# The first projection of a mixture of experts by Strassen's scheme: 42 short matmuls in place of 24 long ones

## The reference, cut to what matters

```python
x = x + xattn(layernorm(x), ctx, ...)                      # first part: not changed
t = layer_norm(layernorm(x).reshape(-1, 512), gamma, beta) # 16384 tokens, 512 wide
logits = t @ gate_weight.T                                 # 8 experts
top1 = argmax(logits)                                      # and the rank of a token in its expert
dispatch[top1, slot] += t * keep                           # (8, 1024, 512): at most 1024 tokens an expert
h = gelu(einsum('ech,ehi->eci', dispatch, wi))             # wi: (8, 512, 2048)   first projection
expert_out = einsum('eci,eih->ech', h, wo)                 # wo: (8, 2048, 512)   second projection
x = x + (residual + weight * expert_out[top1, slot])
```

## Time and profile before

| | |
|---|---|
| Median of 3 runs | 3422.04 us (3421.35 to 3423.3) |
| The profiled execution's own time | 3423.79 us |
| Its span | 3422.0 us |
| PE busy | 3297.7 us (96%), 15632 matmuls |
| DVE busy | 2557.8 us (75%) |
| ACT busy | 1773.7 us (52%) |
| POOL busy | 1383.0 us (40%) |

### The profile page before, as it was taken

How to read it: one execution, slowest core, us unless ns; L and a number is a source line. 1 busy time by engine, 2 the same in 40 slices (tenths; PEclk the granted TensorE clock), 3 DMA queues, 4 the chain that set the end, 5 groups by cost and what they waited for, 6 DMA issues and landing times. The chain is left out here.

```text
span 3422.0 us, 48582 instructions
## 1 busy us (share of the span) xinstructions
PE 3297.7 (96%) x15632; PEld 2611.4 (76%) x15632; DVE 2557.8 (75%) x3185; ACT 1773.7 (52%) x3622; POOL 1383.0 (40%) x1608
## 2 busy tenths in 40 slices
PE   6999999999999999999999589999999999999998
PEld 5777777777777777777777368888888888888886
DVE  4999999999999999999999644444444444444443
ACT  5666666676766666666666343333333333333332
POOL 3476767676776767676775500000000000000000
PEclk9999999999999999999999789999999999999999
DMA  6422222222121222212130232333333333233231
GB/s 226 148 100 75 88 74 63 76 72 86 62 86 62 93 68 86 87 62 74 62 100 31 76 130 99 111 124 115 118 123 120 113 123 110 98 111 113 97 110 37
DMA packets 223806, 325.82 MB, mean 95 GB/s; under 512 B 37104, under 2 KB 103024, under 8 KB 223728
## 3 DMA queue, kind: packets, MB, share of 16 engines
q1 hardware_dynamic: 208368, 307.85, 26.7%
q0 software_dynamic: 15360, 16.99, 1.5%
HBM read 256.70 MB, written 101.97 MB: 105 GB/s over the span
## 5 line engine op out<-in xcount | busy, mean ns | idle before, releaser
L1458 ACT ACTIVATE act<-hid_ps 128x512 f32<-128x512 f32 x256 | 153.1, 598 | 796.3 <-PE hid_ps L1385 796.3
L1339 POOL TENSOR_TENSOR tally<-tally,unit 1x1 f32<-1x1 f32 x16 | 2.9, 180 | 1348.2 <-DVE mixed L1531 1348.2
L1519 DVE CAST act_h<-act 128x512 fp32r<-128x512 f32 x256 | 109.2, 427 | 522.0 <-ACT act L1458 522.0
L1385 PE MATMUL hid_ps<-tok_h,w_h 128*128 128x512 f32 x1024 | 404.9, 395 | 0.0
L1385 PE MATMUL hid_ps<-tok_l,w_h 128*128 128x512 f32 x1024 | 399.3, 390 | 0.0
L1385 PE MATMUL hid_ps<-tok_h,w_l 128*128 128x512 f32 x1024 | 398.7, 389 | 0.0
L1401 PE MATMUL out_ps<-w_l,act_h 128*128 128x512 f32 x1024 | 398.5, 389 | 0.0
L1399 PE MATMUL out_ps<-w_h,act_h 128*128 128x512 f32 x1024 | 398.3, 389 | 0.0
L1400 PE MATMUL out_ps<-w_h,act_l 128*128 128x512 f32 x1024 | 398.3, 389 | 0.0
L1513 DVE TENSOR_TENSOR w_l<-w_raw,w_h 128x2048 fp32r<-128x2048 f32 x128 | 293.4, 2293 | 90.9 <-ACT w_h L1452 90.9
L1452 ACT ACTIVATE w_h<-w_raw 128x2048 fp32r<-128x2048 f32 x128 | 244.5, 1910 | 8.9 <-PEq L311 8.9
(11 more groups left out here) (196 smaller groups left out, 8762.2 us busy)
## 6 DMA issues: line engine op xcount, KB each, us to landing
w_raw<-in_L_ffn_wi SPq DMA_DIRECT2D x128, 512.0 KB, 3.6
w_raw<-in_L_ffn_wo SPq DMA_DIRECT2D x128, 512.0 KB, 4.5
w_raw<-in_x SPq DMA_DIRECT2D x32, 1024.0 KB, 5.1
w_raw<-in_ctx SPq DMA_DIRECT2D x32, 1024.0 KB, 5.2
x_res<-in_x SPq DMA_DIRECT2D x31, 1024.0 KB, 5.3
out<-x_res SPq DMA_DIRECT2D x31, 1024.0 KB, 4.4
slots<-rows SPq DMA_DIRECT2D x4, 4160.0 KB, 16.0
got<-slots SPq DMA_DIRECT2D x15, 1040.0 KB, 7.4
```

The source lines that it names most:

```text
L1339: nc.gpsimd.tensor_tensor(tally[:], tally[:], unit[:], ALU.add).then_inc(tallied, 1)
L1385: last = nc.tensor.matmul(hid_ps[i % 2][:], a[:, c, :], b[:, c, :], start=first_, stop=last_)
L1458: nc.scalar.activation(act32[i % 2][:], hid_ps[i % 2][:], ACT.Gelu).then_inc(gelu, 1)
L1519: v.tensor_copy(act_h[i % 4][:], act32[i % 2][:]).then_inc(ah_ready, 1)
```

## The change

The first projection of a group now goes in 8 steps of 256 inner columns. The weights of a step and the tokens are cut into 2x2 blocks, each 128 inner columns (of the two halves of the 2048) by 256 of the contraction, and 256 of the contraction by 256 tokens. Strassen's scheme (in the form with 15 additions) forms four sums of weight blocks, `S1` to `S4`, and four of token blocks, `T1` to `T4`, and takes seven block products in place of eight. A product is 2 blocks of the contraction by 3 terms, that is 6 matmuls of 256 columns. The products accumulate in four banks, `x_ps`, `y_ps`, `w_ps` and `v_ps`; where a partial sum is needed twice, ACT copies it from bank to bank (`seed_x`, `seed_w`) or to memory (`keep_fifth`), and DVE makes two last additions (`add_22`, `add_12`). The transposes go through one bank, shared with `v_ps`, in place of two. ACT makes all high parts, DVE all low parts. `mixed` goes; the result is written over `res`, and the columns for the scatter come by a small transfer of their own (`meta_of`).

For a step `q` the PE list is: `P1`, `P5`, then `P4` of step q-1, `down` tile 0 of step q-2, `P6`, `P2`, `down` tile 1, `P7`, `P3`, `down` tiles 2 and 3. A tile of `down` is now 6 matmuls of 512 columns, since a step has 256 inner columns.

```diff
-ISTEPS = INNER // P
-PAIRS = ISTEPS // 2
+HALF = INNER // 2
+STEPS = HALF // P
+TOK = GROUP // 2
+INNER_RING = 2
+BLOCKS = 7
@@ load_weights
+    for h in range(2):
+        at = h * HALF + k * P
+        sp.dma_start(raw[:, 0, h * 512:(h + 1) * 512].rearrange("p (c n) -> p c n", c=CB),
+                     wi[bass.ds(e, 1), :, at:at + P].rearrange("a (c p) n -> p (a c) n", p=P)).then_inc(raw_in[k % 2], 16)
@@ PE
+                def product(dst, q, i, a, b, start=False):
+                    g, w = i // STEPS, i % 2
+                    for k in range(2):
+                        for x, y in ((wi_h, tok_h), (wi_l, tok_h), (wi_h, tok_l)):
+                            last = nc.tensor.matmul(dst, x[w][:, a, k, :], y[g][:, b, k, :],
+                                                    start=start and k == 0 and x is wi_h and y is tok_h, stop=False,
+                                                    skip_group_check=True)
+                    return last
...
+                def first_products(q, n, i):
...
+                    pe.wait_ge(wi_low, q * 2 + 2)
+                    wait(pe, sum12, q)
...
+                    product(y_ps, q, i, A11, B11, start=True).then_inc(p1_mm, 1)
...
+                    product(v_ps, q, i, S1, T1, start=True).then_inc(p5_mm, 1)
+                def last_product(q, i):
+                    pe.wait_ge(sum22, q + 1)
+                    product(w_ps, q, i, A22, T4).then_inc(p4_mm, 1)
+                def sixth_product(q, i):
+                    pe.wait_ge(seeded_x, q + 1)
+                    product(y_ps, q, i, S2, T2).then_inc(p6_mm, 1)
+                def second_product(q, i):
+                    product(x_ps, q, i, A12, B21).then_inc(p2_mm, 1)
+                def late_products(q, i):
+                    pe.wait_ge(seeded_w, q + 1)
+                    product(w_ps, q, i, S3, T3).then_inc(p7_mm, 1)
+                    product(y_ps, q, i, S4, B22).then_inc(p3_mm, 1)
@@ ACT, one step
+                    seed_x(q, i)                     # x_ps <- y_ps, 256 columns
+                    keep_fifth(q, i)                 # fifth <- v_ps, 256
+                    inner_high(q - 1, before, 0)     # 512
+                    gelu_21(q - 1)                   # 256
+                    inner_high(q - 1, before, 1)     # 512
+                    weights_high(q + 1, after)       # 768
+                    seed_w(q, i)                     # w_ps <- y_ps, 256
+                    gelu_11(q)                       # 256
+                    weight_sums_high(q + 1, after)   # 1024
+                    down_weights_high(q + 1, after)  # 1024
+                    gelu_22(q)                       # 256
+                    gelu_12(q)                       # 256
+                    if j == 0:
+                        norm(n + 1, 1 - g)           # 4 x 512
+                    if 1 <= j <= CB:
+                        affine(n + 1, j - 1)         # 512
+                    if j == 3:
+                        tokens_high(n + 1, 1 - g, 0) # 1024
+                    if j == 4:
+                        residual(n, g, (0, 1, 2))    # 3 x 512
+                    if j == 5:
+                        tokens_high(n + 1, 1 - g, 1) # 512
+                        tokens_high(n + 1, 1 - g, 2) # 1024
+                        residual(n, g, (3,))         # 512
+                    if j == 6:
+                        tokens_high(n + 1, 1 - g, 3) # 1024
@@ DVE, one step
+                    weights_add(q + 1, after, 0)     # 2 x 256
+                    weights_add(q + 1, after, 1)     # 2 x 256
+                    inner_low(q - 1, before, 0)      # 512
+                    if j == 2:
+                        mix(n - 1, 1 - g, (2, 3))    # 2 x 512
+                    if on(q):
+                        if j == 4:
+                            tokens_low(n + 1, 1 - g, 0)  # 1024
+                        if j == 5:
+                            tokens_add(n + 1)            # 4 x 512
+                        if j == 6:
+                            tokens_low(n + 1, 1 - g, 1)  # 512
+                            tokens_low(n + 1, 1 - g, 2)  # 1024
+                        if j == 7:
+                            tokens_low(n + 1, 1 - g, 3)  # 1024
+                    inner_low(q - 1, before, 1)      # 512
+                    if j == 1:
+                        mix(n - 1, 1 - g, (0,))      # 512
+                    weights_low(q + 1, after)        # 768
+                    weight_sums_low(q + 1, after)    # 1024
+                    add_22(q, i)                     # 256
+                    add_12(q, i)                     # 256
+                    down_weights_low(q + 1, after)   # 1024
+                    if j == 1:
+                        mix(n - 1, 1 - g, (1,))      # 512
```

More of the change, by code:

```diff
@@ L1354, in _, with mark_banks, turn @@
             def _(pe):
-                def turn(e, g, c):
-                    n = group(e, g)
+                def mark_banks():
+                    for bank in (x_bank, w_bank):
+                        for a in range(2):
+                            nc.tensor.matmul(bank[:, a * P:(a + 1) * P], eye[:], eye[:],
+                                             start=(a == 0), stop=True, skip_group_check=True)
+                def turn(n, c, q):
+                    if not group_on(n):
+                        return
                     first = isinstance(n, int) and n == 0
@@ new lines, in _ @@
+                weights_high(0, 0)
+                weight_sums_high(0, 0)
+                down_weights_high(0, 0)
+                norm(0, 0)
+                affine(0, 0)
+                affine(0, 1)
+                affine(0, 2)
+                affine(0, 3)
+                tokens_high(0, 0, 0)
+                tokens_high(0, 0, 1)
+                tokens_high(0, 0, 2)
+                tokens_high(0, 0, 3)
+                for i in range(16):
+                    step(0, i)
+                with act.Fori(1, EXPERTS - 1) as e:
+                    for i in range(16):
+                        step(e, i)
@@ L1498, in _ @@
+                for i in range(16):
+                    step(EXPERTS - 1, i)
+                step(EXPERTS, 0)
             @block.vector
@@ new lines, in _ @@
+                weights_add(0, 0, 0)
+                weights_add(0, 0, 1)
+                weights_low(0, 0)
+                weight_sums_low(0, 0)
+                down_weights_low(0, 0)
+                tokens_low(0, 0, 0)
+                tokens_add(0)
+                tokens_low(0, 0, 1)
+                tokens_low(0, 0, 2)
+                tokens_low(0, 0, 3)
+                for i in range(16):
+                    step(0, i)
+                with dve.Fori(1, EXPERTS - 1) as e:
+                    for i in range(16):
+                        step(e, i)
@@ L1560 @@
+                for i in range(16):
+                    step(EXPERTS - 1, i)
+                for i in range(3):
+                    step(EXPERTS, i)
 def kernel(**inputs):
```

523 lines of the change are left out of this document (337 added, 186 removed).

## The result

The kernel before took 3422.04 us (median of 13 runs on the same chip), the changed one 3416.04 us (13 runs, 3411.25 to 3419.26). One run of the kernel before was a slow one, at 3732.36 us; the other twelve lie between 3421.35 and 3424.19, and the ratio uses fast runs alone. The ratio is 0.9979, with a 95% interval of 0.9971 to 0.9986: faster by 0.2%, where 1.7% was forecast (3363 us, range 3338 to 3412). Of the 59 us that were forecast 6 came. The profiled run took 3416.19 us, its span is 3414.4; the earlier trace rows have 3422.0.

The account below looks back on a forecast made before the run. The prediction took PE's sum of matmul pitches as the bound: 3422.0 - 69.1 (shorter steps) + 12 (start) - 2 (end) = 3362.9, so 3363 us, range 3338 to 3412.

Parts of the forecast that it names:

- the likeliest case: Experts' part: PE's pitch, 0.1133 to 0.125 us for 256 columns, sets the time, all else hidden; 3345 to 3407, chance 0.75.
- Nothing waits: Experts' part: PE has no gap; 384 matmuls make 87.05 of a group's 89.05 us, so only PE's sum counts.
- p, the pitch of 256 columns: Short fp32r matmuls on PE: 0.1167 us each, between readings of 0.1133 and 0.1200, saving 69.1 us over 128 steps.
- Change between 256 and 512 columns costs nothing that I can see.: PE's row changes between short and long matmuls: each length keeps its own pitch, at no cost.
- The 2.0 us left for transposes: Each group on PE: 16 transposes and what they disturb take 2.0 us, before and after the change.
- The start: Ahead of the first product: serial lists make it 9.0 us late, with later waits and half clock 12 us more.
- The end: After the last matmul: one mix is left in place of four, 2.0 us less.
- ACT and DVE hidden: Experts' part: ACT takes 8.05 and DVE 8.56 of a 10.34 us step, so both stay under PE.
- the wait at step 5: Step 5 of a group: add_12 ends at 10.4 against 10.34 us; costed at nothing, at most 8 us.
- Rival 2: Experts' part: the order on ACT and DVE becomes the bound; for example 48 us lost, 3411; chance 0.12.
- Rivals 3 and 4: Short matmuls: weight load not hidden, 3747 us, chance 0.09; or bare stream at 0.110 us, 3327 us, chance 0.04.
- The estimate of 0.1092 us: Short matmuls on PE: pitch by the skill's formula N / 2.4 + 2.5 ns, which would save 109 us.

Follow-up runs that it names:

- e1: The changed kernel with the loop over experts 1 to 6 written out on SP, PE, ACT and DVE: 3393.89 us.
- e5: The changed kernel with the loop over experts written out on PE alone: 3391.97 us.
- e6: The changed kernel with the loop kept on PE alone, written out on ACT, DVE and SP: 3416.48 us.
- e11: The changed kernel, loops kept, with 32 unused 8x8 matmuls put ahead of the experts' part: 3397.97 us.
- e13: As e11, and in an expert's last step two late products go ahead of the second down tile, so 18 long matmuls end the loop's body: 3394.18 us.
- e4: The kernel before, loops written out, each 512-column matmul of the first projection cut into two of 256 columns: 3464.81 us.
- e10: The kernel before, loops written out, each 512-column matmul of the first projection cut into four of 128 columns: 4124.28 us.
- e7: As e1, with P6 and P2 moved ahead of down tile 0, so a step has two rows of long matmuls, not three: 3391.79 us.
- e12: The changed kernel, loops kept, with 64 unused 8x8 matmuls put ahead of the experts' part: 3414.42 us.

## Why the prediction was wrong

The side was right (0.86 for faster), and the likeliest case was the right mechanism: PE's sum of pitches, with ACT and DVE hidden. The time lies outside the range of 3338 to 3412. Of the 51.5 us between 3414.4 and the forecast span of 3362.9, 22.7 lie in the plain groups, 22.8 in the turns and 6.0 in the start.

- **A term that was not there: the turn of the loop** (22.8 us). This is the step that failed. "Nothing waits: this part is the sum of PE's pitches, and only that sum, or a wait that the change makes, can move its end" looked for waits between engines and in transfers. The change also makes PE's loop longer, 1088 pairs for 800, and that was never counted, though both counts follow from its own numbers (48 and 66 matmuls a step). e1, e5 and e6 show the place, e11 to e13 both gaps. Shown. Without the turns the changed kernel takes 3393.89 us (e1), inside the range; the other misses, 28.7 us together, would not have left it.
- **p, the pitch of 256 columns**, taken at 0.1167 as "the middle of the two likely readings". It is the upper reading, 0.120: 336 x 3.7 ns = 1.22 us a group, 19.5 us. The fp32 rows, of which it says "That speaks for growth with the columns", misled; the note that fp32r is another mode was the better guide. A middle between two readings of which one must be true is a value that neither gives. Shown by e4.
- **"Change between 256 and 512 columns costs nothing that I can see."** The long ones average 0.2302 in place of 0.2267: 192 x 3.5 ns = 0.68 us a group, 10.9 us. Seen in every trace with mixed rows, e4 too; its cause is open.
- **The 2.0 us left for transposes** were 1.42, and 0.48 that belonged to the long ones near them; in the sum this gives 7.7 us back (16 x 0.48, against the 1.90 of a plain group before).
- **The start**, 12 us forecast, 18.0 measured. The lists up to the first product were right within about 1 us (8.0 for 9.0). The table load (1.28 us) and the wait of the second step for its sums of weights were not laid out. The end was right.
- **ACT and DVE hidden**: right. ACT is busy 70% of the long window (78% forecast), DVE 71% (83%), PE waits for neither after 2012 us, and the wait at step 5, costed at nothing, costs nothing. Rival 2 falls. The sum for ACT had a slip: the list of a step has seven instructions of 256 columns, not six, so it should have read 6.77 and with the group's share 8.43 of 10.34 us. That both engines were busy for less than their sums fits the overlap of neighbours by some 0.08 us, which the forecast had read from `mix`. (The worth of the change at p = 0.125 is 24.3 us, not 24.6; nothing hangs on it.)
- **Rivals 3 and 4**: the load is hidden at 256 columns and is the bound at 128 (e10); no short matmul is at 0.110. The estimate of 0.1092 us that the forecast worked out from the Trainium skill (TensorE: Matmul & The Clock Gate, section Back-to-back issue gap), which gives the formula for an isolated matmul, does not hold for this format; 0.120 does.

## What to carry to other kernels

Before replacing long instructions by more and shorter ones in a loop, count the instructions of the loop's body on that engine, and ask whether it still fits: here 800 pairs did and 1088 did not. A long branch at the loop's end and traffic on the instruction queue between its turns show in a trace that it does not. If it must be fetched again, end the body with instructions long enough that those already queued cover the branch (here 17 x 0.2267 us for 3.6), and have its first instructions not at the end of a piece; or write the loop out. With that, the change is worth 0.9% (e5, 3391.97 us; e7 the same) and not 0.2%; with the loop kept and only moved and reordered, it is worth 0.8% (e13).

## What the runs showed of the hardware

- 64 unused pairs of load and matmul far ahead of a loop made the kernel some 18 us faster (e11), 128 of them changed nothing that can be told (e12: ratio 0.9979, as without them), by where the loop then lay.
- Of the ten gaps of 2.1 to 3.2 us between starts at the turns of the changed kernel and of e12, seven were followed by some matmuls at 1.2 GHz (0.213 us for 256 columns); three, of 2.1 to 2.3 us, were not.
- fp32r with fresh weights: 0.2267 us at 512 columns, 0.120 at 256, 0.112 at 128.
